# ScalarE's transpose copies moved behind the projection copies, first values in another bank, and expert regions filled ahead, in an attention and mixture-of-experts kernel

## The reference

```python
def attn(x, Wq, Wk, Wv, Wo, gamma, beta):          # 16 heads of 64
    q, k, v = (einsum('bsd,hde->bhse', x, W) for W in (Wq, Wk, Wv))
    scores = where(causal, (q @ k.T) / sqrt(64), -inf)
    heads = (softmax(scores) @ v).transpose(0, 2, 1, 3).reshape(B, S, H * E)
    y = x + heads @ Wo
    return (y - mean(y)) * rsqrt(var(y) + 1e-3) * gamma + beta

def ffn(x, router_w, w1, w2):                      # 8 experts, top 2, hidden 512
    probs = softmax(x @ router_w)
    top_p, top_i = top_k(probs, 2)
    for e in range(8):
        gate_e = sum(where(top_i == e, top_p, 0))
        out += gate_e * (gelu(x @ w1[e]) @ w2[e])
    return out

x = x + layernorm(attn(layernorm(x), ...))
x = x + layernorm(ffn(layernorm(x), ...))
```

## Time and profile before

| | |
|---|---|
| runs | 707.39, 707.59, 709.84 us |
| profiled execution | 707.34 us, its span 705.6 us |
| PE busy | 677.8 us (96%) |
| ACT busy | 552.3 us (78%) |
| DVE busy | 547.0 us (78%) |
| POOL busy | 281.6 us (40%) |
| granted TensorE clock, mean | 0.996 |
| DMA moved | 34.89 MB |

### The profile page before, as it was taken

The page is one execution under the profiler, slowest core; times in us unless marked ns, Lnnn a source line. Parts: engine busy times, 40 slices in busy tenths (PEclk is TensorE's granted clock), DMA queues, the critical chain, the costliest instruction groups (busy, mean ns, idle before and its releaser), DMA issues.

```text
span 705.6 us, 18101 instructions
## 1 busy us (share of the span) xinstructions
PE 677.8 (96%) x5762; PEld 576.4 (82%) x5763; DVE 547.0 (78%) x2557; ACT 552.3 (78%) x1815; POOL 281.6 (40%) x424
## 2 busy tenths in 40 slices
PE   6999999999999999999999999999989999999994
PEld 5788878888878888788888788888878999999951
DVE  5677798989899898989898888888897774444326
ACT  5888888889898888888898988888885664555515
POOL 3012234343434353432323231423213777755545
PEclk9999999999999999999999999999999999999998
DMA  7900000000000000000000000000020243322155
GB/s 170 280 9 9 9 9 25 16 25 9 25 9 25 8 26 14 19 25 17 25 8 24 10 24 9 24 13 14 22 66 27 70 118 113 104 76 76 51 196 181
DMA packets 40537, 34.89 MB, mean 49 GB/s; under 512 B 10528, under 2 KB 36128, under 8 KB 40448
## 3 DMA queue, kind: packets, MB, share of 16 engines
q1 hardware_dynamic: 34816, 23.81, 12.5%
q0 software_dynamic: 4544, 9.45, 3.8%
q10 hardware_dynamic: 1088, 0.54, 0.3%
HBM read 20.22 MB, written 13.56 MB: 48 GB/s over the span
## 4 chain that ended last, share of the span: by engine, by line
PE 70%; ACT 20%; DMA 3%; DVE 2%; issue 2%; POOL 1%; DVEq 0%; SPq 0%; POOLq 0%; ACTq 0%
PE PT1O L446 13%; PE SC L434 9%; PE M L704 9%; PE M L411 6%; ACT qk L1308 5%; ACT pT L1328 5%; ACT prob L1319 5%; PE M L413 4%; PE M L412 4%; PE SC L437 4%; PE A L457 4%; ACT pT L1325 3%; PE PT1O L465 3%; PE SC L411 3%; PE SC L412 2%; PE SC L413 2%
## 5 line engine op out<-in xcount | busy, mean ns | idle before, releaser
L808 DVE CUSTOM_DVE_ANT_0 SC<-SC,mask 128x128 f32<-128x128 f32 (+1 forms) x512 | 166.0, 385 | 3.8 <-PE SC L437 3.3
L1319 ACT ACTIVATE prob<-SC,nmax 128x256 f32<-128x256 f32 x256 | 135.6, 530 | 0.0
L1308 ACT ACTIVATE qk<-M 128x512 f32<-128x512 f32 x127 | 77.6, 611 | 54.7 <-PE M L413 54.7
L446 PEld LDWEIGHTS PT1O<-pT,v_sb 128*64 128x64 f32 x1024 | 63.4, 136 | 49.1 <-ACT pT L1328 30.5
L1313 ACT ACTIVATE prob<-SC,nmax 128x128 f32<-128x128 f32 x256 | 101.9, 420 | 1.5 <-DVE nmax L808 1.5
L446 PE MATMUL PT1O<-pT,v_sb 128*64 128x256 f32 (+1 forms) x1024 | 97.3, 332 | 5.2 <-ACT pT L1328 0.9
L820 DVE TENSOR_TENSOR prob<-prob,rden 128x512 f32<-128x512 f32 x128 | 89.7, 700 | 2.4
L1610 POOL DMA_INDIRECT expert_rows<-v_sb,got x74 | 73.2, 990 | 36.2 <-ACT v_sb L1470 17.5
L1599 POOL DMA_INDIRECT sent_rows<-rec,slot x64 | 64.8, 1013 | 51.3 <-DVE slot L1074 34.9
L434 PE MATMUL SC<-qk 64*128 64x256 f32 x512 | 83.5, 403 | 0.9 <-ACT prob L1319 0.6
L411 PE MATMUL M<-xt_hi,wqk_hi 128*128 128x256 f32 x254 | 83.2, 328 | 1.2 <-ACT v_sb L1332 0.8
(11 more groups left out here) (212 smaller groups left out, 1731.3 us busy)
## 6 DMA issues: line engine op xcount, KB each, us to landing
got<-sent_rows SPq DMA_DIRECT2D x39, 132.0 KB, 2.3
w_in<-expert_rows SPq DMA_DIRECT2D x8, 512.0 KB, 4.9
x_in<-L_attn_x SPq DMA_DIRECT2D x16, 128.0 KB, 2.1
w_in<-L_ffn_w SPq DMA_DIRECT2D x1, 2048.0 KB, 12.4
x_res<-L_attn_x SPq DMA_DIRECT2D x16, 128.0 KB, 2.1
w_sb<-L_ffn_w SPq DMA_DIRECT2D x8, 256.0 KB, 4.6
out<-prob SPq DMA_DIRECT2D x6, 256.0 KB, 2.1
sent_rows<-pad_rec SPq DMA_DIRECT2D x11, 132.0 KB, 4.8
```

Of the source, the lines that this page charges most:

```text
L446: last = mm(PT1O[k * E:(k + 1) * E, cols], v_sb[:, t, h * E:(h + 1) * E], src[:, par, k, :], start=(t == 0), stop=(t == 1), skip_group_che ...
L808: last = v.tensor_tensor_reduce(SC[par][:, k, cols], SC[par][:, k, cols], m, -1.0, -MASKED, ALU.add, ALU.min, nmax[:, par, late, k:k + 1])
L1308: a.activation(qk[:, p % 2], src[:].rearrange("p (i s) -> p i s", i=2), ACT.Copy).then_inc(qk_sb, 1)
L1319: return a.activation(prob[:, slot, k, 1:3, :].rearrange("p n t -> p (n t)"), SC[par][:, k, LATE_Q], ACT.Exp, scale=-1.0, bias=nmax[:, par ...
```

## The change

Six things change.

1. In every step but the first, ScalarE's order is changed: the two copies of a pair's transposes now stand directly behind the copy of a projection, and both `exps_late` of pair p stand behind the second pair of transpose copies.
2. In the first step, the first values go into bank `PT0`, which is empty then, and PE no longer waits for two copies there; ScalarE takes two exponentials before its first copy.
3. One of the four weight roundings (the second half of Wk) moves from ScalarE to GpSimd; VectorE's `qk_low` waits for it there.
4. In the last attention step, `first_rows` stands ahead of both transposes on PE.
5. The pads are gone from both queues. In their place SyncE fills all regions with pad records while attention runs: 16 DMAs `fill_st`, each of 256 rows of each of 8 experts (1.08 MB), issued behind each batch's `x_res` load. Each waits for the one before, and `send(r)` waits for fill r.
6. A tile's 256 rows are laid out as (p t) instead of (t p), so that a partition's two rows are adjacent in memory (one run of 1056 bytes instead of two of 528).

```diff
@@ sync: batch(b), load_tiles, pads
-                        sp.dma_start(rows.rearrange("(t p) c -> p t c", p=P), pad_rec[:, k])\
+                        sp.dma_start(rows.rearrange("(p t) c -> p t c", p=P), pad_rec[:, k])\
...
+                for j in FILLED[b] if b < B else ():
+                    if j == 0:
+                        sp.wait_ge(sem("pad_ok"), 2)
+                    else:
+                        sp.wait_ge(sem("fill_st"), 16 * j)
+                    sp.dma_start(regions[:, j * ROWS:(j + 1) * ROWS, :].rearrange("e (p t) c -> p e (t c)", p=P),
+                                 pad_rec[:].rearrange("p e t c -> p e (t c)"))\
+                        .then_inc(sem("fill_st"), 16)
...
-            def pads():
-                sp.wait_ge(sem("pads_known"), 1)
...
-                for e in range(NE // 2):
-                    sp.dma_start(sent[bass.ds(rows[e], ROWS), :].rearrange("(t p) c -> p t c", p=P), pad_rec[:, e])\
-                        .then_inc(sem("pad_st"), 16)
...
-            pads()
...
-            sp.wait_ge(sem("pad_st"), 16 * NE)
@@ tensor: step(b, u)
+                if is_last(b) and u == STEPS - 1:
+                    first_rows()
                 if k >= 1:
                     pe.wait_ge(nrm, p - 1)
...
                 if k == 0:
-                    pe.wait_ge(qk_sb, 3)
-                    v_proj(0, 0)
+                    v_proj(0, 0, PT0)
...
                         w_o((c - 3) % NP)
-                        first_rows()
...
                     pe.wait_ge(qk_sb, p + 3)
-                    if k == 0:
-                        pe.wait_ge(v_done, 1)
                     qk_proj((c + 3) % NP)
@@ scalar: step(b, u)
+                if k == 0:
+                    exps_early(p, 0)
+                    exps_late(p, 0)
                 if more:
                     qk_copy(p + 2)
-                exps_early(p, 0)
                 if k == 0:
-                    v_copy(1, 0, 0)
-                if k >= 1:
+                    v_copy(1, 0, 0, PT0)
+                else:
                     pT_copies(p - 2)
-                exps_late(p, 0)
+                    exps_early(p, 0)
                 if more:
                     qk_copy(p + 3)
-                exps_late(p, 1)
                 if k >= 1:
                     pT_copies(p - 1)
+                if k >= 1:
+                    exps_late(p, 0)
+                exps_late(p, 1)
                 exps_early(p, 1).then_inc(exp_done, 1)
...
-                    if n == 10:
-                        pads[:] = pad_rows()
-                        store_pads(NE // 2, 3 * NE // 4)
-                    if n == 11:
-                        store_pads(3 * NE // 4, NE)
@@ gpsimd
+            pool.wait_ge(wk_ld[1], 16)
+            q.tensor_copy(wqk_hi[:, 1, half_cols(1)], wqk_in[:, 1, half_cols(1)]).then_inc(sem("wk_h"), 1)
...
                 pool.wait_ge(sem("rec_ok"), r + 1)
+                pool.wait_ge(sem("fill_st"), 16 * (r + 1))
```

More of the change, by code:

```diff
@@ L55, in sandwich_kernel @@
     back = nc.dram_tensor("expert_rows", (K * N + (NE + UNUSED) * ROWS, D), F32, kind="Internal").ap()
+    regions = sent[0:NE * CAP, :].rearrange("(e c) d -> e c d", e=NE)
     back_groups = back[0:K * N, :].rearrange("(g p r k) d -> g p r k d", g=NG, p=P, r=K)
@@ L221, in sandwich_kernel @@
         LAG = 2
+        FILLED = [[], [], [0], [1, 2], [3, 4]] + [[b] for b in range(5, B)]
+        assert sum(FILLED, []) == list(range(N // ROWS))
         STEPS = NP // 2
@@ L321, in batch @@
                     sp.dma_start(x_res[:], x_tiles[b - 1]).then_inc(sem("x_res_ld"), 16)
-                if isinstance(b, int) and b < 2:
+                if b < 2:
                     expert_weights(b)
+                for j in FILLED[b] if b < B else ():
[6 more added lines that the diff above has]
+                        .then_inc(sem("fill_st"), 16)
             def table_values(row, largest, why):
@@ L336, in load_tiles @@
                         sp.wait_ge(back_st[k], 32 * it)
-                    sp.dma_start(got[:, k], sent[bass.ds(rows[k], ROWS), :].rearrange("(t p) c -> p t c", p=P))\
+                    sp.dma_start(got[:, k], sent[bass.ds(rows[k], ROWS), :].rearrange("(p t) c -> p t c", p=P))\
                         .then_inc(got_ld[k], 16)
-            def pads():
-                sp.wait_ge(sem("pads_known"), 1)
-                sp.wait_ge(sem("pad_ok"), 2)
-                rows = table_values(pad_row[0:1, :], NE * CAP - ROWS,
-                                    "an expert gets N rows at most, its region has CAP")
-                for e in range(NE // 2):
-                    sp.dma_start(sent[bass.ds(rows[e], ROWS), :].rearrange("(t p) c -> p t c", p=P), pad_rec[:, e])\
-                        .then_inc(sem("pad_st"), 16)
             over_batches(batch)
@@ L828, in qk_low @@
                     scale = (float(E) ** -0.5, 1.0)[i]
-                    dve.wait_ge(sem("wqk_h"), 2 * g + i + 1)
+                    if g == 1 and i == 1:
+                        dve.wait_ge(sem("wk_h"), 1)
+                    else:
+                        dve.wait_ge(sem("wqk_h"), 2 * g + i + 1)
                     v.scalar_tensor_tensor(wqk_lo[:, i, cs], wqk_in[:, i, cs], scale, wqk_hi[:, i, cs].bitcast(F32),
@@ L1328, in pT_copies, with v_copy @@
                 a.activation(pT0[:, p % 2], PT0[:].rearrange("p (k s) -> p k s", k=2), ACT.Copy).then_inc(pt0_sb, 1)
-            def v_copy(n, t, half_of_heads):
+            def v_copy(n, t, half_of_heads, src=M):
                 act.wait_ge(v_mm, n)
-                a.activation(v_sb[:, t, half_of_heads * 512:half_of_heads * 512 + 512], M[:], ACT.Copy)\
+                a.activation(v_sb[:, t, half_of_heads * 512:half_of_heads * 512 + 512], src[:], ACT.Copy)\
                     .then_inc(v_done, 1)
@@ L1357, in qk_high @@
                 for i, (loaded, scale) in enumerate(((wq_ld[g], float(E) ** -0.5), (wk_ld[g], 1.0))):
+                    if g == 1 and i == 1:
+                        continue
                     act.wait_ge(loaded, 16)
@@ L1433, in between @@
                     records(B - 1)
-            pads = []
-            def pad_rows():
-                act.wait_ge(sem("pads_known"), 1)
-                act.wait_ge(sem("pad_ok"), 2)
-                return nc.values_load_multi_w_load_instructions(
-                    pad_row[0:1, :], engines=[mybir.EngineType.Activation], min_val=0, max_val=NE * CAP - ROWS,
-                    skip_runtime_bounds_check_because="an expert gets N rows at most, its region has CAP")[1]
-            def store_pads(first, end):
-                for e in range(first, end):
-                    nc.scalar.dma_start(sent[bass.ds(pads[e], ROWS), :].rearrange("(t p) c -> p t c", p=P), pad_rec[:, e])\
-                        .then_inc(sem("pad_st"), 16)
             def gelu(n, s, halves=range(2)):
@@ L1640, in batch @@
             def batch(b):
-                if isinstance(b, int) and b == LAG + 1:
+                if b == 2:
                     pool.wait_ge(sem("spare_st"), 16 * UNUSED)
```

8 lines of the change are left out of this document (3 added, 5 removed).

## The result

The changed kernel takes 711.14 us (median of six runs, 709.64 to 711.65); the kernel before, beside it, 707.65. The ratio is 1.0041, with a 95% interval of 1.0027 to 1.0056. On another chip it was 1.0038 (1.0023 to 1.0053). So it is 0.4% slower, by 2.9 us on average, where 706.4 was forecast (704.5 to 708.5): outside the range, and on the other side of no change.

A forecast was written before the change was run, and what follows sets the result against it. PE was busy 96%; a plain step's chain ran through ScalarE to the value product, then PE. Terms -1.7 + 0.6 + 1.65 - 1.5 = -0.95 from 707.34 gave 706.4 us; range 701.5 to 710.5, the forecast's own 704.5 to 708.5.

The forecast's parts named there:

- the first step: First attention step: PE starts the second projection sooner, waiting only for one copy, so scores(1) comes 1.74 us earlier; -1.7.
- step 1: Attention step 1, which has no w_o and no idle time ahead of the second copy: down to 7.8 us, -0.5.
- the plain step: Attention steps without additions: ScalarE idles ahead of the second projection's copy, 8.00 us instead of 7.90, 45 steps, +4.5.
- The fills: Pad records written during attention: cost 0, or 4.3 us of a transfer with 20 us of slack if ahead of a send.
- (b): Rival, attention: a second ScalarE restart, transpose copies also wait for PE; plain step 8.11, +5.0, total 711.4; chance 0.14.
- (a): Rival, attention: second projection's copy is not waited for, plain steps 7.75, -11 more, total 695.2 (half way 701); chance 0.18.
- (c): Rival, last attention step: costs nothing because the first rows come sooner; total 704.7; chance 0.10.
- (d): Rival, attention: reordering does nothing since PE's own work binds; total 705.8; chance 0.58 together with the forecast.
- Step 1 that failed: Attention steps u = 1: bound by PE, lose only the 0.22 wait at the second transposes; 8.30 instead of 8.52, 13 times, -2.9.
- The same step, its second part: GpSimd's rounding in the first step: no row shows a copy blocked by VectorE's shared port; nothing in the sum, bound +1.
- Step 2 that failed: Last attention step: PE waits for first rows ahead of pair 124's transposes, pair 127's start later; +1.65, bounds 0 and +2.3.
- Step 3 that failed: Expert stage, tile 16: without pads the last send starts and lands sooner, rows arrive at 587.7 instead of 589.23; -1.5.

The follow-up runs named there:

- e4: Kernel before with only fills in place of pads and the (p t) layout of a tile's rows: 0.9971 of the kernel before.
- e3: Kernel before with only the first values in bank PT0, two exponentials ahead of the first copy, one rounding on GpSimd: 0.9984 of the kernel before.
- e10: Changed kernel with GpSimd's split_w1(b, 1) moved behind send(b - 3): 1.0010 of the kernel before, against 1.0038 for the changed kernel beside it.
- e1: Changed kernel with first_rows put back behind w_o in the last attention step: 0.9999 of the kernel before.
- e2: Kernel before with only ScalarE's new order, in every step but the first: 1.0050 of the kernel before.
- e6: Changed kernel with 24 unused products keeping PE busy ahead of the wait for the first rows in the last attention step: 1.0019 of the kernel before.
- e8: Kernel before with only first_rows ahead of both transposes in the last attention step: 1.0022 of the kernel before.
- e5: Kernel before with transpose copies early but exps_late(p, 0) kept ahead of the second projection's copy, steps 1 to 62: 0.9882 of the kernel before.
- e11: Changed kernel with tile 8's store ahead of the last send on GpSimd: 1.0033 of the kernel before.
- e9: The changed kernel again, unaltered, measured on one chip with other follow-up kernels: 1.0038 of the kernel before.

## Why the prediction was wrong

Of the 4.9 us between the forecast and the profiled execution, 1.9 lie in steps 2 to 61, 1.5 in the last step, 1.2 at tiles 16 and 17, and 0.3 ahead of step 0 and behind tile 17.

**Right, to a few hundredths:** the first step (-1.74 forecast, -1.72 measured), step 1 (-0.5, -0.45), the plain step: where ScalarE would stand idle, S + 1.82, S + 6.08 and 6.12 (6.05 and 6.10 measured), and 8.00 against 7.96 measured. The wait moved to `scores(1)` as told. The fills cost no step anything (e4), and the first step's gain is kept through attention (e3). The last send lands in 2.27 us without the pads, as forecast. Of the rivals, (b) was not it: a plain step is not 8.11. That the total came out near its 711.4 is chance. Nor were the others: the second copy is waited for (a), PE waits for the first rows (c), and the steps did change (d).

**Step 1 that failed: u = 1 steps at 8.30.** I took 0.22 of idle time at the second transposes as all removable, since it vanishes when ScalarE's copy comes first. Then VectorE's normalisation is next, also where GpSimd is not beside it. In step 37:

```profile
313.11 0.42 DVE L823 TENSOR_TENSOR prob<-prob,rden 128x256 f32<-128x256 f32 x1
...
313.58 0.20 PEld L467 LDWEIGHTS PT1O<-ident,prob 128*128 128x128 f32 x2
```

The normalisation ends 0.05 ahead of the transposes' weight load, at S + 1.65, so they start at S + 1.70, only 0.08 sooner than before (313.33 - 311.55 = 1.78). In step 13, where PE waits 0.28, it is S + 1.89, and in step 9, without such a wait, S + 1.55. The steps take 8.44, 8.64 and 8.34, so 6.74 to 6.79 follow that start in each, as they did before (8.52 - 1.78). The 13 steps are +0.2 in sum where -2.9 was forecast. That is 3 us, more than the whole error of this line (1.9), since the 45 others came out cheaper than forecast (+3.2 instead of +4.5). I had asked what is late next on ScalarE, and not on VectorE.

**The same step, its second part: what GpSimd does to VectorE.** The prediction said that no row shows a blocked copy, and I had looked for one only in the first step. VectorE's six additions of 0.27 instead of 0.17 us were in the trace of before. In the changed kernel they are 0.20 too long (once 0.29) and on the path; e10 takes just that away and gains 1.37 us of attention. The Trainium skill (SBUF — State Buffer, "SBUF: two separate sides") says that a VectorE operation with two SBUF inputs and a GpSimd operation that reads SBUF lock each other out of a shared port pair for a whole instruction. The trace agrees: the addition has two such inputs and ends 0.02 us behind GpSimd's subtraction.

**Step 2 that failed: the last step, +1.65 forecast, +3.13 measured.** Three terms stand in its place. The new order costs 1.0 there without any early rows (e1: 1.84 - 0.88 behind the kernel before, e2: 3.94 - 2.97); this was in my sum, and put down to `first_rows`. The wait for the rows costs 0.6 to 0.8 (e6 against e1; e8: 0.82). The granted clock at 0.50 costs 1.5 to 1.6: from S of step 62 to tile 2's transposes it is 24.39 us in the changed kernel, 22.79 in e6, and 22.91 in e10, which has the same last step and in whose profile the clock did not fall there. Before it was 21.26, so e10 is at +1.65, my forecast (to the hundredth by luck, since its rows come 0.19 sooner behind S than the changed kernel's); what I had left out is the clock. I named waits of 2 us, and took the time of all matmuls behind them from rows at full clock. Tile 16 shows the same price: it takes 5.10 to 5.12 us in the three profiles with a fall there (e3, e6, e8), and 3.52 or 3.53 before, in e2, e5 and e11.

**Step 3 that failed: tile 16, -1.5 forecast, -0.31 measured.** In e4 the tile starts 0.94 sooner, not 1.5: I had taken the third send's 1.7 us to be the pads' doing, let the last send start 0.8 sooner and tile 8's stores end at 585.6. But the third send takes 1.72 without pads too, what stands behind it starts where it did (the last send at 581.23, before 581.19; the last store of tile 8 at 583.76, before 583.71), and the load goes out at 586.14. Then tile 17's load has to wait for tile 9's store, and 0.25 is left at tile 18. I had followed the chain to one tile and not to the next.

**What stays open.** In the profiles the clock fell behind idle times of PE of 1.70 (changed kernel), 1.74 (e9), 1.62 (e11), 2.08 (e3), 2.11 (e8, tile 16) and 1.87 (e6, tile 16). It did not fall behind 2.01 (e8, last step), 2.22 (e2, tile 16), 1.51 with 0.32 soon behind it (e10, last step), 1.49 (e11, tile 16), 1.47 (before) and 1.39 (e5). So an idle time of 1.6 us or more stands ahead of each fall, and where it was filled (e6, last step) there was no fall behind it in the profile; why some of the same size let it pass is not settled by these runs. How much of the changed kernel's loss over many executions is the clock stays open too, since its fall is seen in profiles alone.

## What to carry to other kernels

When an engine's order is changed to bring one result forward, write down for each wait of that engine when it arrives and when the other side is ready. Here ScalarE arrived 0.1 us too early and stood idle for 0.24, all of it on the chain behind, and one more instruction moved in front of the wait won it back: that is the difference between 7.97 and 7.75 us a step, and most of the 1.7% between e2 and e5. Then ask what is late next on every engine that feeds the step, and for the next tile as well as for this one. Where a change brings a new wait of PE of 1.6 to 2.2 us, as here, price it twice, with full clock behind it and with some 1.5 us more.

## What the runs showed of the hardware

- Behind some idle times of TensorE of 1.6 us and more, the granted clock was 0.50 for 3.4 us in each profile where it fell, at 1.5 to 1.6 us of lost time (e6, e10, and tile 16 in e3, e6 and e8). With 24 small products in the gap it stayed at 1.00 in e6's profile.
- With the mean clock the runs of the kernel before fall into two groups some 2 us apart (on one chip: 707.9 to 709.2 at 0.995 to 0.997, and 709.8 to 710.9 at 0.993 to 0.995). Not every kernel shows this: e1 spreads from 708.6 to 711.0 and e6 from 709.1 to 711.4 at 0.995 to 0.997. That shorter waits move a median by moving runs from one group into the other fits e4 (2 us by the ratio, 0.3 at tile 18 in the profile), and is not shown.
- PE's idle time ahead of the 16 weight loads of a value product is nowhere under 0.35, whoever is named, and 0.35 to 0.37 in all but one of the 63 in e5: 0.37 "ACT" in the earlier trace rows, and in the same step after the change, with the copies done long before:

```profile
315.98 1.28 PEld L448 LDWEIGHTS PT1O<-pT,v_sb 128*64 128x64 f32 x16 [0.36 <-issue]
```

- An addition of VectorE of 8 columns took 0.17 us alone, 0.27 where a rounding of GpSimd of 128 columns had started 0.05 us ahead of it, and 0.37 or 0.46 where a subtraction of 128 columns had started 0.02 to 0.11 ahead; each time it ended 0.02 or 0.03 behind GpSimd's instruction.
- Sixteen writes of 1.08 MB beside attention, which took 4.6 to 6.9 us each to land, did not lengthen one step by more than 0.02 us (e4).
- The last send landed 4.81 us after its start beside the pads, and 2.27 or 2.28 without them (changed kernel, e4, e9, e10).
